# A recommendation tower on Trainium2: turning the Gram's 32x32 blocks straight out of PSUM

## What is computed

```python
e = jnp.stack([tbl_0[ids[:, 0]], ..., tbl_26[ids[:, 26]]], axis=1)      # 2048 x 27 x 128
dot = jnp.einsum('bnd,bmd->bnm', e, e)                                  # the Gram of each sample
z = dot.reshape(2048, 27 * 27)[:, pairs_i_below_j]                      # 351 pairs
h = jnp.concatenate([z, dense_ctx], axis=1)
h = jnp.maximum(h @ W_top1 + b_top1, 0.0)                               # 367 -> 512
h = jnp.maximum(h @ W_top2 + b_top2, 0.0)                               # 512 -> 256
y = h @ W_top3                                                          # 256 -> 1
```

## Time and profile before

| | |
|---|---|
| Median of 3 runs | 703.17 us (702.69 to 704.76) |
| The profiled execution | 701.53 us, its span 699.7 us |
| Busy: TensorE matmul / weight load | 392.1 us (56%) / 344.1 us (49%) |
| Busy: VectorE / ScalarE / GpSimd | 257.3 us (37%) / 157.7 us (23%) / 263.0 us (38%) |
| Mean granted TensorE clock | 0.741 of full |
| HBM read | 35.39 MB, 51 GB/s over the span |

### The profile page before, as it was taken

One profiled execution on the slowest core, in us unless ns is written; L12 is line 12 of the kernel. 1 busy time (PEld: TensorE's weight loads), 2 busy tenths in 40 slices (PEclk: granted clock), 3 DMA queues, 4 the chain that ended last, 5 costly groups with the idle time before them and its releaser, 6 DMA issues.

```text
span 699.7 us, 15045 instructions
## 1 busy us (share of the span) xinstructions
PE 392.1 (56%) x6064; PEld 344.1 (49%) x6064; DVE 257.3 (37%) x733; ACT 157.7 (23%) x212; POOL 263.0 (38%) x281
## 2 busy tenths in 40 slices
PE   3216332595437926297154954289361982559875
PEld 3116231593326915197143944179151971439754
DVE  5305122482134714085041921257140850417121
ACT  2407210032111402033020322014020330203321
POOL 6770547106371074503562064701645035630000
PEclk9657656597567966599575986679675895759998
DMA  8924311111121121111111211211111121110000
GB/s 202 232 53 122 94 31 50 47 50 41 24 53 44 48 53 28 45 32 65 45 38 28 75 38 30 53 39 50 49 34 41 32 65 45 38 27 2 2 2 1
DMA packets 22699, 35.77 MB, mean 51 GB/s; under 512 B 12921, under 2 KB 13569, under 8 KB 22674
## 3 DMA queue, kind: packets, MB, share of 16 engines
q0 software_dynamic: 8832, 18.11, 10.2%
q1 hardware_dynamic: 13842, 17.32, 9.0%
HBM read 35.39 MB, written 0.01 MB: 51 GB/s over the span
## 4 chain that ended last, share of the span: by engine, by line
PE 51%; issue 37%; another core or an unknown queue 4%; ACT 4%; DVE 2%; DMA 2%; SPq 1%; DVEq 0%; ACTq 0%
PE emb_ps L641 19%; PE gram_ps L672 14%; PE mlp_ps L691 5%; PE emb_ps L664 5%; PE mlp_ps L705 4%; DMA turned<-in_tbl 2%; PE mlp_ps L734 1%; PE mlp_ps L713 1%; DVE onehot L531 1%; PE mlp_ps L682 1%; ACT parts L398 1%; ACT embT L415 1%; PE mlp_ps L739 1%; SPq L253 1%
## 5 line engine op out<-in xcount | busy, mean ns | idle before, releaser
L376 POOL DMA_INDIRECT rows<-in_tbl,idx x272 | 258.9, 952 | 354.4 <-PE emb_ps L664 239.7
L672 PE MATMUL gram_ps<-embT 128*32 128x26 f32 x4096 | 99.5, 222 | 248.2 <-issue 244.6
L672 PEld LDWEIGHTS gram_ps<-embT 128*32 128x32 f32 x4096 | 78.2, 143 | 272.6 <-issue 269.7
L641 PE MATMUL emb_ps<-onehot,parts 125*128 125x256 f32 x1248 | 165.9, 292 | 47.3 <-issue 43.2
L531 DVE TENSOR_SCALAR onehot<-ids_b,row_of 128x256 fp32r<-128x256 int32 x608 | 167.3, 355 | 50.3 <-remote 29.2
L641 PEld LDWEIGHTS emb_ps<-onehot,parts 125*128 125x128 f32 x1248 | 159.7, 198 | 50.2 <-issue 44.7
L543 DVE COPY blocks<-gram_ps 128x416 f32<-128x416 f32 x16 | 14.6, 910 | 293.6 <-PE gram_ps L672 293.6
L444 ACT ACTIVATE blocks<-gram_ps 128x416 f32<-128x416 f32 x16 | 14.2, 885 | 333.5 <-PE gram_ps L672 333.5
L415 ACT ACTIVATE embT<-emb_ps 128x512 f32<-128x512 f32 x40 | 48.1, 1224 | 102.5 <-PE emb_ps L641 102.5
L537 DVE COPY embT<-emb_ps 128x512 f32<-128x512 f32 (+1 forms) x32 | 33.3, 1046 | 58.3 <-PE emb_ps L664 54.4
L419 ACT ACTIVATE embT<-emb_ps 128x512 f32<-128x512 f32 (+1 forms) x48 | 45.8, 1067 | 10.0 <-PE emb_ps L664 7.0
(11 more groups left out here) (37 smaller groups left out, 104.6 us busy)
## 6 DMA issues: line engine op xcount, KB each, us to landing
ids_b<-in_ids_mm SPq DMA_DIRECT2D x8, 768.0 KB
rows<-in_tbl,idx POOLq DMA_INDIRECT x272
ids_b<-in_ids_mm SPq DMA_DIRECT2D x16, 256.0 KB, 3.4
turned<-in_tbl SPq DMA_DIRECT2D x6, 448.0 KB
h<-in_tbl SPq DMA_DIRECT2D x2, 448.0 KB
blocks<-in_tbl SPq DMA_DIRECT2D x2, 448.0 KB
w_sb<-in_W_top SPq DMA_DIRECT2D x1, 512.0 KB, 6.8
w_sb<-in_W_top SPq DMA_DIRECT2D x2, 224.0 KB
```

What stands on the lines that cost most here:

```text
L376: pool.indirect_dma_start(rows[:, t, n, :], None, tables[f], bass.IndirectOffsetOnAxis(idx[:, t, f:f + 1], 0), engine_sem=gathers_written) ...
L641: last = nc.tensor.matmul(emb_ps[BANK[k]][:, m * W:(m + 1) * W], parts[0:MP, f, part, c * D:(c + 1) * D], onehot[0:MP, f % OH, c, :], star ...
L672: last = nc.tensor.matmul(gram_ps[s][q * COLS:(q + 1) * COLS, g * NJ:(g + 1) * NJ], embT[:, t, at:at + COLS], embT[:, t, at:at + NJ], star ...
```

## The change

The two banks become one PSUM tensor `gram_ps` of 32 x 32 columns over both banks, the columns of a sample group at a distance of 32 in place of 26. `gram` is one step. The copies by VectorE and ScalarE, `blocks` and two semaphores go. VectorE's transpose reads PSUM itself: within a block its 32 elements lie 32 columns apart. `turn` is split: `flip` (the transpose) stands where VectorE's copy stood, `fill_z` (the other three instructions) where `turn` stood. `turned` has one buffer for both tiles; the staging buffers get memory of their own.

```diff
-        blocks = sb("blocks", [P, TILES, NJ, G], F32)
-        turned = sb("turned", [P, TILES, JEXT * 32], F32)
+        turned = sb("turned", [P, JEXT * 32], F32)
+        stages = sb("stages", [P, 2, CH * D], F32)
...
-        gram_ps = [ps(f"gram_ps{k}", [P, 512]) for k in range(STEPS)]
+        gram_ps = ps("gram_ps", [P, G * COLS])
...  ScalarE, at the end of a tile
-                    keep_blocks(p, t, 1)
...  VectorE
-                dve.wait_ge(gram_dve, p * TILES + t + 1)
-                dve.wait_ge(gram_act, p * TILES + t + 1)
-                past(dve, s_z, (p - 1) * TILES + t + 1)
-                nc.vector.transpose(turned[:, t, 0:NJ * G], blocks[:, t, :, :].rearrange("p j g -> p (j g)")
+            def flip(p, t):
+                dve.wait_ge(gram_filled, p * TILES + t + 1)
+                past(dve, s_z, p * TILES + t)
+                nc.vector.transpose(turned[:, 0:NJ * G], gram_ps[:].rearrange("p (g j) -> p j g", g=G)[:, 0:NJ, :]
                                     ).then_inc(s_turned, 1)
+            def fill_z(p, t):
                 dve.wait_ge(s_turned, p * TILES + t + 1)
...
                             if last and t and k == 3:
-                                turn(p, 0)
+                                fill_z(p, 0)
                             move_rows(p, t, k)
                     if t and not last:
-                        turn(p, 0)
+                        fill_z(p, 0)
                     if not last and not first:
                         make_onehot(p + 1, t)
-                    keep_blocks(p, t, 0)
+                    flip(p, t)
                     if first:
                         make_onehot(p + 1, 2 * (1 - t))
                         make_onehot(p + 1, 2 * (1 - t) + 1)
-                turn(p, 1)
+                fill_z(p, 1)
...  TensorE
-            def gram(p, t, s):
-                past(pe, (gram_dve, gram_act)[s], p * TILES + t)
-                for g in range(GS):
+            def gram(p, t):
+                past(pe, s_turned, p * TILES + t)
+                for g in range(G):
                     for q in range(Q):
-                        at = ((GS * s + g) * Q + q) * SLOT
-                        last = nc.tensor.matmul(gram_ps[s][q * COLS:(q + 1) * COLS, g * NJ:(g + 1) * NJ],
+                        at = (g * Q + q) * SLOT
+                        last = nc.tensor.matmul(gram_ps[q * COLS:(q + 1) * COLS, g * COLS:g * COLS + NJ],
```

More of the change, by code:

```diff
@@ L86 @@
 Q, G = 4, 32
-GS = 16
-STEPS = G // GS
 SHIFTS, RUN = NF // 2, 9
@@ L158, in dlrm_tower @@
         y_last = sb_view(early_rows, W, [[1, W]], 0, 1)
-        stage = [turned[:, t, 0:CH * D] for t in range(TILES)] + [
-            sb_view(h1, 0, [[1, CH * D]]), sb_view(blocks, 0, [[1, CH * D]])]
+        stage = [stages[:, 0, :], stages[:, 1, :], turned[:, 0:CH * D], sb_view(h1, 0, [[1, CH * D]])]
         emb_ps = [ps(f"emb_ps{k}", [P, 512]) for k in range(EMB_BANKS)]
-        gram_ps = [ps(f"gram_ps{k}", [P, 512]) for k in range(STEPS)]
+        gram_ps = ps("gram_ps", [P, G * COLS])
         mlp_ps = [ps(f"mlp_ps{k}", [P, 512]) for k in range(2)]
@@ L193, in dlrm_tower @@
         gram_filled = sem("gram_filled")
-        gram_dve = sem("gram_dve")
-        gram_act = sem("gram_act")
         s_turned = sem("s_turned")
@@ L253, in load_in_two @@
                     eng.dma_start(dst[a:b, :], src[a:b, :]).then_inc(landed, 16)
-        def block_views(t, s):
-            src = gram_ps[s][:, 0:GS * NJ].rearrange("p (g j) -> p g j", g=GS)
-            return sb_view(blocks, t * NJ * G + GS * s, [[1, GS], [G, NJ]]), src
         block = ctx.enter_context(nc.Block())
@@ L437, in move_y @@
                 nc.scalar.activation(y[:], mlp_ps[1][0:1, 0:W], ACT.Copy).then_inc(mlp_moved, 1)
[L439 to L444, removed]
             def last_layers(kind, t):
@@ L537, in move_rows @@
                 nc.vector.tensor_copy(*row_views(t, k)).then_inc(emb_dve, 1)
[L539 to L545, removed]
-                dve.wait_ge(gram_dve, p * TILES + t + 1)
-                dve.wait_ge(gram_act, p * TILES + t + 1)
-                past(dve, s_z, (p - 1) * TILES + t + 1)
-                nc.vector.transpose(turned[:, t, 0:NJ * G], blocks[:, t, :, :].rearrange("p j g -> p (j g)")
+            def flip(p, t):
+                dve.wait_ge(gram_filled, p * TILES + t + 1)
+                past(dve, s_z, p * TILES + t)
+                nc.vector.transpose(turned[:, 0:NJ * G], gram_ps[:].rearrange("p (g j) -> p j g", g=G)[:, 0:NJ, :]
                                     ).then_inc(s_turned, 1)
+            def fill_z(p, t):
                 dve.wait_ge(s_turned, p * TILES + t + 1)
[L555 to L559, removed]
+                nc.vector.tensor_copy(turned[:, NF * 32:], turned[:, 0:SHIFTS * 32]).then_inc(s_ext, 1)
+                nc.vector.tensor_copy(sb_view(turned, NJ * 32 + NJ - SHIFTS, [[1, SHIFTS]]),
+                                      sb_view(turned, (NJ - SHIFTS) * 32 + NJ, [[32, SHIFTS]])
                                       ).then_inc(s_ext, 1)
@@ L562, in turn @@
                 past(dve, mlp_filled, (p - 1) * MLP_JOBS + t + 1)
-                src = sb_view(turned, t * JEXT * 32 + 32, [[33 * RUN, KCH], [32, SHIFTS], [33, RUN]])
+                src = sb_view(turned, 32, [[33 * RUN, KCH], [32, SHIFTS], [33, RUN]])
                 dst = z[:, t, :, 0:PAIRS_CH].rearrange("b c (s r) -> b c s r", r=RUN)
@@ L796, in body @@
                     emb_moved(p, t)
-                    gram(p, t, 0)
-                    gram(p, t, 1)
+                    gram(p, t)
                 if first:
```

## The result

The changed kernel is slower, by about the amount forecast. Its median is 703.92 us (701.36 to 708.12, 20 runs) against 700.63 us for the kernel before on the same chip (697.07 to 706.06, 20 runs): ratio 1.0048, 95% interval 1.0026 to 1.0071, about +3.4 us. The forecast was +0.37%. Its profiled execution took 703.23 us, with a mean granted clock of 0.74.

What follows compares the result with a forecast made beforehand. In passes 0 to 6 the stream of 17 gathers was taken to set each Gram's end. For F = 1.8, 2.60 + 0.2 - 0.19 = +2.6 us on 703.17 gave 705.8 us (+0.37%), eight in ten 702.4 to 708.2.

Steps and rivals of the forecast that it cites:

- The price F: Time of the new transpose reading PSUM with large steps: taken as 1.8 us, with 1.04 as the other end.
- cheap read: Rival: the new transpose costs 1.04 to 1.2 us, so the kernel is +1.0 to +1.4 us; chance 0.32.
- (a): Hand-over from pass 0 to pass 1: one-hots wait for the transpose, +2.60 us for F = 1.8, +1.84 for 1.04.
- (b): Between the Grams of pass 0: second Gram starts about 2.6 us later, hidden by the gathers, cost +0.2 us.
- (c): Passes 1 to 6, 12 tiles: the transpose's delay is used up by idle time, no change.
- (d): ScalarE's 16 removed copies: no gain, since behind each it waits for TensorE again.
- (e): End of pass 7, without cover: faster by 0.19 us for F = 1.8, 0.95 for F = 1.04.
- Faster: Rival: a 2.30 us TensorE stop in the last Gram moves behind it, giving 701.9 or 700.6 us; chance 0.05.
- TensorE's clock: Rival: at pass 1's start it gives back half the delay (+1.3, chance 0.08) or costs more (+5.2; 0.10 with dearer flip).

Runs made afterwards that it cites:

- e7: Kernel before with the Gram's columns 32 apart, and only the very last tile transposed straight out of PSUM, its two copies dropped: 699.33 us, ratio 0.9974.
- e8: Kernel before with pass 0's one-hots ahead of the copies, with the crawl: 696.03 us, ratio 0.9922.
- second pair: The profiles of the changed kernel and the kernel before, run again unchanged with the crawl: medians 704.48 us against 702.06, ratio 1.0031.
- e3: Kernel before, with VectorE's copy in pass 0 held back until the whole Gram is done, no crawl: 393.94 us, ratio 0.9998.
- e1: Changed kernel with pass 0's one-hots ahead of the transpose, no crawl: 396.60 us against 393.87 for the kernel before, ratio 1.0048.
- e5: Changed kernel run again as it is, with the crawl: 704.48 us against 702.06 for the kernel before, ratio 1.0031.
- e6: Kernel before run again as it is, with the crawl, one run with a profile: 702.75 us.
- e9: Changed kernel with 76 semaphore instructions ahead of TensorE's program, no crawl: median 405.85 us, 6 runs, no ratio.
- e11: Changed kernel with pass 0's one-hots ahead of the transpose and 76 instructions ahead of TensorE's program, no crawl: 408.80 us, ratio 1.0262 to the kernel before.
- first pair: The profiles of the first measurement: changed kernel 703.23 us (median 703.92) beside the kernel before (median 700.63), ratio of the kernels 1.0048.
- e10: Changed kernel with pass 0's one-hots ahead of the transpose, repeated without the crawl: 396.69 us, ratio 1.0037 to the kernel before.
- e4: Kernel before with only the Gram's columns 32 apart in one PSUM tensor, copies kept, no crawl: 393.89 us, ratio 0.9975.
- e12: Kernel before with only the Gram's columns 32 apart in one PSUM tensor, repeated without the crawl: 393.35 us, ratio 0.9991.
- e2: Kernel before with pass 0's one-hots ahead of the copy, no crawl: 395.12 us, ratio 1.0014.

## Why the prediction came out as it did

The time and its sign were right: +2.6 us forecast, +3.4 measured, in the range. That the number came out is in good part luck. The transpose's price was put 0.75 us too high, which made the sum 1.6 us too high, and two terms were missing, a second stop of +2.5 us and a shorter gather, worth -1.1. The narrow range given with the 705.8 (704.5 to 707.2) doesn't follow from the scatter named for it either, which would give 705.3 to 707.4.

- **The price F failed.** I took 1.8 us; it is 1.05 (16 of 16 in the changed kernel, 1.06 in e7). The argument went by the nearest shape: scattered writes from PSUM cost 1.95 ns per column, so scattered reads might too. They don't: 832 elements read 32 columns apart go at the rate of contiguous ones. The copy into z, which reads scattered and gave 1.16 us, was the row to believe. Of the two rules weighed there, the Trainium skill's warning on non-contiguous PSUM elements (Advanced Engine Details and Errata, PSUM Cachelines) doesn't show in this transpose; the cycle table (VectorE: DVE Perf Modes, the section on the TRN2 errata) would give +65 ns as an estimate, and +10 was measured. With the cheap read the sum would have been +1.0 us.
- **(a) The hand-over** held at that end: +1.84 forecast for F = 1.04, +1.95 measured (5.33 against 3.38 us, counted from the Gram's end), and e8 shows that this wait is on the path when the Grams crawl, and costs more than its length. About half of it was given back by the shorter gather ahead of it, so that the lookup itself came 0.88 us later, and 1.11 in the second pair. e3 shows no cost when the gathers set the pace. With the crawl, neither e3's edit nor the changed kernel without the hand-over (e1) was run, so +1.95 is read from the traces and wasn't undone by a run.
- **(b) Between the Grams of pass 0** held: the second Gram started 2.3 us later (108.93 against 106.64), waited 4.94 us where it had waited 2.46, and ended 6.0 us behind the end of the last gather, where before it was 5.7 (6.1 and 5.6 in e5 and e6). What the prediction took as fixed, the length of the gather stream, wasn't: its first gather took 2.14, 2.15 and 2.60 us in the three kernels with the crawl in which VectorE's copy stands ahead of the one-hots (before, e6, e7), and 0.94 to 0.95 in the changed kernel, in e5 and in e8. With one-hots first, as in e8, it is as short as behind the new transpose. The cause stays open. (Four records in each 0.75 us are 14 in 2.6 us, not 12; the +0.2 stays.)
- **(c) and (d), passes 1 to 6 and ScalarE:** held, by pass 3 and by the pass lengths. The part on what bounds the kernel puts the end of a Gram 3.3 us behind the gathers; there its last burst starts, and it ends 6.2 us behind (351.62 against 345.40). All but 1 us of the 27.5 us of busy time that went was in shadow.
- **(e) The end of pass 7** held at the cheap end: -0.95 forecast for F = 1.04, -0.96 measured in the first pair, -0.95 between e5 and e6, and -0.96 by itself in e7.
- **The missing terms** are the shorter gather under (b) and the last Gram's second stop, +2.5 us in the first pair and +3.1 between e5 and e6. My rival *Faster* had the right object, a stop in TensorE's code, and the wrong sign, and it counted a shift of 6 instructions. There is none: both kernels show 12,466 instructions of TensorE in the trace (e9 and e11 12,542, 76 more). The packets of the queue that brings instructions show what differs: in the kernel before one started 2.5 us ahead of the last Gram, and one more 1.9 us into it; in the changed kernel none came shortly ahead, and two came in it, at 0.9 and 4.7 us. So it is in all twelve profiles without the shift: the seven with one stop have a packet 1.9 to 2.5 us ahead of the last Gram, the five with two have none there, and two in it, at 0.9 to 1.1 and 4.4 to 4.9 us. The place 140 records from the end is there in both kernels; the packets fit that its code is late in only one.
- **TensorE's clock** as a rival played next to no part in the changed kernel: after the longer wait the first lookup of pass 1 took 6.17 us at a mean granted clock of 0.61, before 6.37 at 0.59; in the second pair it was 5.74 at 0.67 against 5.42 at 0.72. Of the kernels run with the crawl only e8, with next to no pause, had it at 1.00 (4.04 us).

How sure is the second stop as part of the change? It appeared in all 4 profiled executions with TensorE's program as changed and without the shift (first measurement, e1, e5, e10), in one of the two with the layout alone (e4, not e12), in none of the 6 others (before, e2, e3, e6, e7, e8), and in none of the two shifted. That ties it to the changed kernel, but not to a line of it, and e4 shows that it can come and go with one and the same program. Why the early fetch is missing stays open, and no run took the stop out of the changed kernel with the crawl. Without it the change would be +1.0 us by the hand-over and the end, about nothing with the shorter gather: not to be told from no change either way.

The fastest kernel of these runs with the crawl is e8, which keeps the copies and only moves pass 0's one-hots: 696.0 us, against 702.1 before and 704.5 for the changed one. The change with that move was timed only without the crawl, where it is 0.4 to 0.5% slower than the kernel before.

## What to carry to other kernels

Busy time removed from an engine is worth what the next instruction in its queue, and whoever waits for that, gets earlier: here 27.5 us of copies were worth 1 us, at the one place without cover, and a step that merged two waits into one later wait cost twice that at a hand-over. When an instruction must wait for more than the one that it replaces, look first at what stands behind it in its queue; with the crawl, moving pass 0's one-hots ahead of VectorE's copy was worth more (-5.5 us) than the whole change. A difference of 0.5% in one kernel may be code that arrives late: compare where the stops without a cause fall, before giving the time to the edit. And a sum of terms that meets the measured time isn't proof that none is missing: compare when the same instruction starts in both traces, place by place. Here that shows a term of -1.1 us that the sum had left out.

## What the runs showed of the hardware

- One program on one chip took 702 us in one set and 394 in another. With the gathers running, the Grams crawled, in pass 3 at one or two records at a time with idle stretches of 0.5 to 2.6 us between them, or ran at 252 in 4.06 us. Nothing in the kernels differed. In passes 2 to 6 no instruction packets came at all (from 221 to 629 us in the first profiles), so the crawl there is not the fetching of code.
- VectorE's transpose of 832 columns reads PSUM with a step of 32 columns in 1.05 us, contiguous SBUF in 1.04; copies out of PSUM that write 27 words apart go at 1.95 ns per column.
- In the last Gram TensorE stood still for 1.8 to 2.6 us at places 256 instructions apart, and 76 instructions ahead of it moved such a place by 38 matmul records, exactly.
- 32 lookup matmuls behind a pause of 2.6 us took 5.42 us (e6, mean granted clock 0.72) and 6.37 (before, 0.59), behind next to none 4.04 (e8, 1.00).
- The same gather on GpSimd took 0.94 to 1.05 us in five profiles without the crawl and 11.02 and 11.32 in two others (e11, e10).
